# Where the MLP norm's scale and offset are applied, and the order of five queues: a change to a fused two-branch block on one Trainium2 core

## The reference, cut to what matters

```python
xn = _layernorm(x)                       # x: 1 x 4096 x 256
s  = linear_attention(xn)                # 16 heads of 32, softmaxed q and k, decay mask, _ln, W_out
for l in range(2):                       # the local branch, layer l
    h = shift_token(x)
    q, k, v = split(h @ wqkv)            # 8 heads of 64
    q, k = rotary_xpos(l2norm(q) * qs, l2norm(k) * ksc)
    x = x + local_attention(q, k, v) @ wo        # windows of 128, look back one window
    h = shift_token(x)
    h = (h - mu) / sqrt(var + 1e-5) * lg + lb    # the MLP norm
    a, g = split(h @ w1 + b1)
    x = x + (a * gelu(g)) @ w2 + b2
out = x0 + s * silu(x)
```

## Time and profile before

| | us |
|---|---|
| runs | 2031.31, 2036.61, 2037.25 |
| median | 2036.61 |
| profiled execution | 2033.74 |
| its span | 2031.7 |
| TensorE busy | 1933.6 |
| VectorE busy | 1733.0 |
| ScalarE busy | 1169.2 |
| GpSimd busy | 1015.4 |

### The profile page before, as it was taken

How to read it: one execution, slowest core, us unless ns; L and a number is a source line. 1 busy time by engine, 2 the same in 40 slices (tenths; PEclk the granted TensorE clock), 3 DMA queues, 4 the chain that set the end, 5 groups by cost and what they waited for, 6 DMA issues and landing times.

```text
span 2031.7 us, 49195 instructions
## 1 busy us (share of the span) xinstructions
PE 1933.6 (95%) x15282; PEld 1663.3 (82%) x15282; DVE 1733.0 (85%) x5322; ACT 1169.2 (58%) x2798; POOL 1015.4 (50%) x1005
## 2 busy tenths in 40 slices
PE   5899999999999999999999999999999999999997
PEld 3788888888888888888888888888888888888886
DVE  5788888988888988888876898888899888899885
ACT  3456655655655665655654566566566556556553
POOL 2455455656455655455543455444455453455451
PEclk8799999999999999999998999999999999999998
DMA  5010010010000010000120111110111110111100
GB/s 196 17 32 20 26 31 19 30 31 18 29 27 25 25 31 19 30 26 29 53 86 17 43 32 41 34 31 28 41 31 41 34 31 28 41 32 40 34 28 24
DMA packets 81153, 72.76 MB, mean 36 GB/s; under 512 B 13485, under 2 KB 74345, under 8 KB 81097
## 3 DMA queue, kind: packets, MB, share of 16 engines
q1 hardware_dynamic: 81096, 72.05, 11.7%
HBM read 42.64 MB, written 16.78 MB: 29 GB/s over the span
## 4 chain that ended last, share of the span: by engine, by line
PE 65%; DVE 21%; issue 9%; ACT 2%; POOL 1%; DVEq 1%; SPq 0%; DMA 0%; ACTq 0%; POOLq 0%
PE bank L1477 31%; PE bank L1482 20%; PE bank L1489 10%; PE bank L1534 3%; DVE prob L1022 2%; DVE rot L1377 2%; DVE rot L1387 2%; DVE sq_sum L1351 2%; DVE gel L1241 1%; DVE hid L1260 1%; DVE prob L1041 1%; DVE kT L1213 1%; ACT kT L782 1%; POOL small_y L658 1%; DVE rot_scale L1245 1%
## 5 line engine op out<-in xcount | busy, mean ns | idle before, releaser
L1477 PE MATMUL bank<-hT_n,w_s 128*128 128x128 f32 x3072 | 405.3, 283 | 1.1 <-ACT hT_n L782 0.5
L1477 PEld LDWEIGHTS bank<-hT_n,w_s 128*128 128x128 f32 x3072 | 370.3, 194 | 26.2 <-issue 21.4
L813 ACT ACTIVATE prob<-prob,row_min 128x256 f32<-128x256 f32 x512 | 256.3, 503 | 165.0 <-DVE row_min L1022 164.4
L1482 PE MATMUL bank<-wqkv_s,xT 128*128 128x512 f32 x1152 | 322.0, 416 | 7.3 <-DVE xT L1218 4.7
L701 POOL TENSOR_TENSOR rot_other<-raw,rot_t 128x256 f32<-128x256 f32 x256 | 187.4, 763 | 245.7 <-ACT raw L782 245.7
L658 POOL TENSOR_TENSOR inv_norm<-sq_clip,half_neg 128x8 f32<-128x8 f32 x128 | 242.7, 1906 | 80.2 <-DVE sq_clip L1354 80.0
L1482 PEld LDWEIGHTS bank<-wqkv_s,xT 128*128 128x128 f32 x1152 | 209.9, 193 | 56.4 <-DVE wqkv_s L1195 6.4
L1022 DVE CUSTOM_DVE_ANT_0 prob<-bank,table,inv_norm 128x256 f32<-128x256 f32 x512 | 226.2, 478 | 2.9 <-issue 2.9
L1477 PE MATMUL bank<-w_s,hid 128*128 128x256 f32 x768 | 202.2, 386 | 1.2
L782 ACT ACTIVATE pT<-bank 128x512 f32<-128x512 f32 x256 | 143.4, 604 | 69.4 <-PE bank L1489 69.2
L1534 PEld LDWEIGHTS bank<-kT,qT 64*128 64x128 f32 x1536 | 100.2, 187 | 68.1 <-DVE row_min L1022 34.2
(11 more groups left out here) (184 smaller groups left out, 4297.3 us busy)
## 6 DMA issues: line engine op xcount, KB each, us to landing
k_prev<-k_carry SPq DMA_DIRECT2D x32, 224.0 KB, 2.5
x_s<-in_L_attn_x SPq DMA_DIRECT2D x32, 128.0 KB, 2.0
rot_s<-in_rotary SPq DMA_DIRECT2D x64, 64.0 KB, 2.0
rows_normalised<-xh SPq DMA_DIRECT2D x32, 128.0 KB, 1.7
y_n<-rows_normalised SPq DMA_DIRECT2D x32, 128.0 KB, 2.1
x_between_layers<-x SPq DMA_DIRECT2D x32, 128.0 KB, 1.7
s_between_passes<-s_out SPq DMA_DIRECT2D x32, 128.0 KB, 1.7
x_s<-x_between_layers SPq DMA_DIRECT2D x32, 128.0 KB, 2.0
```

The lines of the kernel that those rows point to most:

```text
L813: ins = act.activation(prob[:, h, :], prob[:, h, :], ACT.Exp, bias=row_min[:, c:c + 1], scale=-1.0, accum_out=row_sum[:, c:c + 1])
L1477: return pe.matmul(out, lhsT, rhs, start=first, stop=last)
L1482: ins = pe.matmul(out, halved(left[:, a]), halved(right[:, b]), start=first and n == 0, stop=last and n == 2)
```

## The change

Five things, in the words of the code.

- ScalarE's copy of `hT_n` becomes two activations (Identity) of 128 x 128 with a scale (gain) and a bias (offset) per partition. Both folds, `b1_s` and the setup events of them are gone; the gates take b1 from `cols`, and the first MLP matmuls of a layer wait for the load of w1 instead of its scaling.
- `norm3` and the store of its rows (SyncE's `store_rows`) move from the end of an iteration into the next one: `norm3` before `scores("b1")`, the store before the DMAs of `k_prev`.
- VectorE: `scores("a0")` before y_n. In odd iterations the sum of squares before p. The low half la before cos. The rotary's addition in two halves; in odd iterations kadd and lb between them. In odd iterations `norm1` and `hidden_tail` behind ql.
- TensorE, even iterations: `state_sum` ahead of `mlp_out(0, 2)` and `turn_q`. `turn_k` directly behind the output projection, ahead of `mlp_out(2, 4)` and the transposes of `go`. ScalarE's copy of k goes before that of `go` accordingly, and its zeroing of kT in the first window of a layer moves forward.
- Where a layer begins: ScalarE cuts the q weights before it copies the transposed rows, and in layer 1 the k and v weights are cut later, on ScalarE after the copy of q and on VectorE after `scores("a1")`.

```diff
-        b1_s = [sb(f"b1_s{l}", [P, 2 * HC]) for l in range(LAYERS)]
...
+        def b1_cols(l):
+            return cols[:, NORM_ROWS + l * 2 * HC:NORM_ROWS + (l + 1) * 2 * HC]
...
+                if 1 <= i.low < NW:
+                    store_rows(i)
                 if mix is not None:
                     sp.wait_ge(mix_pool.sem, mix_pool.at("ksmear", mix))
...
-                if i.low + 1 < NW:
-                    store_rows(i.back(-1))
...
                     act.wait_ge(mlp_pe.sem, mlp_pe.at("ht", m))
-                    copy(hT_n[:, :, :], mlp_bank[1][:, 0:D].rearrange("p (c t) -> p c t", c=DC))\
-                        .then_inc(mlp_act.done("ht"), 1)
+                    gain, offset = norm_cols(6 + 2 * layer(m)), norm_cols(7 + 2 * layer(m))
+                    for c in range(DC):
+                        ins = act.activation(hT_n[:, c, :], mlp_bank[1][:, c * P:(c + 1) * P], ACT.Identity,
+                                             bias=offset[:, c:c + 1], scale=gain[:, c:c + 1])
+                    ins.then_inc(mlp_act.done("ht"), 1)
...
-            def fold(l):
-                dve.wait_ge(setup_pe.sem, setup_pe.at(f"b1_{l}", ONCE))
-                dve.tensor_tensor(b1_s[l][:, :], mlp_bank[0][:, 0:2 * HC], cols[:, at:at + 2 * HC], ALU.add)\
-                   .then_inc(setup_dve.done(f"b1_{l}"), 1)
-                for c in range(DC):
-                    ins = dve.tensor_scalar(w1_s[:, c, :], w1_s[:, c, :], norm_cols(6 + 2 * l)[:, c:c + 1],
-                                            None, ALU.mult)
...
+            def add_other(u, part, name):
+                half = slice(part * E, (part + 1) * E)
+                dve.tensor_tensor(rot[:, half], rot[:, half], rot_other[:, half], ALU.add).then_inc(proj_dve.done(name), 1)
...
+                if a is not None:
+                    scores("a0", a, att_bank[0])
                 if y is not None:
                     dve.wait_ge(mix_pool.sem, mix_pool.at("yrstd", y))
...
+                if 1 <= i.low < NW:
+                    norm3(u)
                 if a is not None:
                     scores("b1", a, att_bank[0])
                 if one is not None:
+                    square_sums(u)
                     dve.wait_ge(mix_pe.sem, mix_pe.at("p", one))
...
-            def fold(l):
-                pe.wait_ge(w1_loaded, 16 * W1_DMAS * (l + 1))
-                for j in range(2 * HC):
-                    for c in range(DC):
-                        ins = mm(mlp_bank[0][:, j:j + 1], w1_s[:, c, j * P:(j + 1) * P],
-                                 norm_cols(7 + 2 * l)[:, c:c + 1], c == 0, c == DC - 1)
...
                     hidden(m, mlp_bank[0], 2, 4, 2).then_inc(mlp_pe.done("ga"), 1)
-                    if one is None:
-                        mlp_out(m, 0, 2)
+                if two is not None:
+                    state_sum(two, 0)
+                    state_sum(two, 1)
+                if m is not None and one is None:
+                    mlp_out(m, 0, 2)
...
                     out_projection(a, att_bank[1])
+                if u is not None:
+                    turn_k(u)
                 if m is not None and two is not None:
                     mlp_out(m, 2, 4)
```

115 lines of the change are left out of this document (54 added, 61 removed).

## The result

The changed kernel takes 2019.4 us (median of 5 runs, 2018.2 to 2022.7) against 2036.6 (5 runs, 2029.5 to 2039.0). The ratio is 0.9926 with a 95% interval of 0.9904 to 0.9949: 10 to 20 us less. The forecast was 1993 us and a range of 1963 to 2015. The sign is right, the size is not, and the time lies outside the range.

The account below looks back on a forecast made before the run. TensorE, busy 95% of the span, was taken as the bound, with VectorE (85%) close behind and the only engine waited for. Once-only savings -30.5, layer 1's loop -23.4 and layer 0's +10 gave -44: 2036.6 to 1993 us, range 1963 to 2015.

Parts of the forecast that it names:

- The second, 8.8 + 3.2: Second fold: its one-column matmuls go, 8.8 us, and the slow-clock stretch behind it, 3.2 us; together 12.0 us saved.
- The first, 8.05 + 2.0: First fold: its one-column matmuls go, 8.05 us, plus 2.0 us from the slow clock behind it; 10.0 us saved.
- The rival of 2032 us: Half the folds' 17 us returns as waits, layer 1 gains nothing, layer 0 loses 10 us; chance 0.05.
- The pair of activations: ScalarE's replacement for the hT_n copy: holds it 0.27 us longer per unit, ends 0 and 0.376, mostly beside other work.
- -15.5: Start to iteration 2: 3.0 us from cutting q first, 2.5 from iteration 1's waits, 10.0 from the first fold.
- I take 3.0 us in all, ends 0 and 8: Where layer 1 begins: row_min's wait goes, kT's shrinks, the slow stretch may shorten; 3.0 us saved.
- I take all 23.4 us, ends 8 and 28: Layer 1's loop: all three of TensorE's waits for VectorE go, 23.4 us saved.
- +10 forecast: Layer 0's loop: 0.4 us from the even and 0.3 from the odd iteration, over 15 pairs; 10 us slower.
- p is some 0.4 us later, and with it tanh, the exponentials and the gelu by 0.15 to 0.3 us: Layer 0's odd iterations: norm3 (0.3 us) and the sum of squares (1.3) before p, where VectorE idles 1.19.
- The rival of VectorE's pace: VectorE sets both loops' pace, each pair 2.2 us longer over 30 pairs, the kernel slower at 2072 us; chance 0.07.
- the own case: Whole kernel: the prediction's main forecast of 1993 us, spanning 1979 to 2007; chance 0.48.
- the main term: The loops' forecast; called wrong if kT's wait is below 9 us in layer 0 or 8.5 or more in layer 1.

Follow-up runs that it names:

- e4: The kernel before with only the folds taken out, ScalarE applying gain and offset in two activations, all orders as before: 2012.0 us, ratio 0.9887.
- e1: The changed kernel with the sums of squares of odd iterations back behind p: 1998.1 us, ratio 0.9814.
- e7: The changed kernel with the squares back behind p and both halves of the rotary addition ahead of kadd: 1992.6 us, ratio 0.9810.
- e8: The changed kernel with squares behind p, both rotary halves ahead of kadd, and four of eight state additions ahead of qT's low half: 1971.1 us, ratio 0.9704.
- e13: The changed kernel with squares behind p, both rotary halves ahead of kadd, and state sums back behind the q transposes: 1975.7 us, ratio 0.9702.
- e17: The kernel before without folds, plus scores a0 and la early, early k transposes and state sums, four state additions ahead of qT's low half: 1969.2 us, ratio 0.9682.
- e6: The changed kernel with the first four of VectorE's eight state additions ahead of qT's low half in even iterations: 2001.1 us, ratio 0.9845.
- e5: The changed kernel with the state sums back behind the q transposes in even iterations: 2008.0 us, ratio 0.9880.
- e16: The kernel before without the folds, with scores a0 ahead of y_n and la ahead of cos on VectorE: 1984.0 us, ratio 0.9740.
- e2: The changed kernel with the first four gated columns ahead of the k half of the rotary addition in odd iterations: 2036.4 us, ratio 1.0013.
- e3: The changed kernel with both halves of the rotary addition ahead of kadd in odd iterations: 2010.3 us, ratio 0.9881.

## Why the prediction was wrong, and what was right

Of the 33 us between the forecast and the profile, 16.7 lie in layer 1's loop, 10 where layer 1 begins and 6.8 in layer 0's loop. The sign is that of the folds: the orders by themselves made the kernel slower.

**The folds.** 22.0 us forecast, 23.2 measured (e4). The second, 8.8 + 3.2, measured 11.7. The first, 8.05 + 2.0, shows 6.7 up to iteration 2 and 1.0 behind it; the rest of e4's gain, 2.8 us, is in the tail behind iteration 63, and belongs to no term. The rival of 2032 us, by which half of that time would come back as waits for other engines, is out. The pair of activations was given 0.27 us with 0.376 as its upper end; it takes 0.80 as one record where the copy took 0.38, 0.42 more, and costs a pair 0.04 to 0.08 us.

**The start.** -15.7 against -15.5, and the agreement is luck. The q cut gave 3.3 (forecast 3.0). In iteration 1 prob's wait fell from 2.9 to 1.6 us and mix_work's rose from 2.2 to 3.3: 0.2 us instead of 2.5. With the squares back behind p (e1) they are 2.9 and 1.0, so the squares are what moved the wait. A new wait of 1.95 us for kT stands before the rows of iteration 2. In all TensorE's idle time fell by 1.6 us, where 5.5 were forecast; its busy time fell by 14.1, of which 8.05 are the fold and 6.0 go with a mean granted clock of 0.92 instead of 0.85, where 2.0 were forecast.

**Where layer 1 begins.** The step "I take 3.0 us in all, ends 0 and 8" failed. The folds alone give 135.4 us from iteration 31 to 35, the change takes 142.1: 6.7 us more, outside its ends. 4.1 of them are idle time of TensorE (7.9 to 12.0), 2.6 busy time. In the view of TensorE's waits of the change, 980 to 1080 us, which answers to the earlier trace rows:

```profile
PE bank L1502 <- DVE mix_work L1406: 3.8, 2, 2.1
PE bank L1495 <- DVE wqkv_s L1205: 3.4, 2, 2.3
PE bank L1490 <- DVE hid L1259: 2.4, 2, 1.2
PE bank L1490 <- ACT gel L930: 2.1, 2, 1.5
```

row_min's and kT's 4.8 us are smaller or gone, 2.3 us of wqkv_s are what the text called "a little later" and gave no price, and the two loops' new waits are larger here than in the loops. With the squares and the split undone, TensorE idles 6.2 to 6.9 us in the stretch (e7, e8, e13) against e4's 7.9: the parts that the step credited save 1.0 to 1.7 us of waiting. The rest is busy time, 126.0 to 129.5 us in these three for nearly the same work, at a mean granted clock of 0.99 in e7 and e13 and 0.96 in e8.

**Layer 1's loop.** The step that failed is "I take all 23.4 us, ends 8 and 28"; measured 5.1 over 14 pairs. The 1.56 us a pair that it stands for can be had: e17 has the moves that were credited, with e6's edit, and is 1.55 below e4. That the two agree to a hundredth is luck, since TensorE's idle time fell by only 1.12 us a pair (a new wait for mix_work, 0.64, stays) and 0.43 are busy time, records that follow each other more closely. What failed is that the other moves of the same change were walked for layer 0 alone. The sum of squares and the split stand in layer 1's odd iterations as well, and cost 0.91 us of the 1.14 between the change and e17; 0.23 lie in what else e7 and e17 differ by.

**Layer 0's loop.** +10 forecast, +16.8 measured, 0.7 against 1.12 us a pair. The even part, state sums ahead of the q transposes, was right in its mechanism and mis-sized: 0.4 forecast, 0.9 measured (e5), and the wait for kT grew to 11.7 us in the stretch of the earlier trace rows, not the 15 that was named. The odd part has one false step: "p is some 0.4 us later, and with it tanh, the exponentials and the gelu by 0.15 to 0.3 us". It was 1.1 us. From start to start, the norm's product holds VectorE for 0.44 us (given 0.3) and the squares with their clip for 1.68 (given 1.3; the clip takes 0.52 instead of 0.17), and VectorE comes to this place 0.24 us later than before. And no one was asked to wait for the gelus: before, they ended 0.35 us before TensorE came for their bank (434.77 + 1.14 = 435.91 against 436.26 in the kernel before), so 0.3 us later was free. They came 0.7 later, and TensorE came 0.46 earlier, which makes 0.8. The delay is 0.87 us, 0.70 of it idle. Undone, the move is worth 1.13 us (e1).

**The k half.** It was given 0.6 us. It takes 1.12 in the iteration shown, since GpSimd's product runs until 0.55 us before its end, and hid came late, a wait the prediction did not have. The rival of VectorE's pace, 7%, had the mechanism and 2.2 us a pair; it set its own decision point at 1.0, and layer 0 passed it with 1.12. Layer 1 did not. The spread of the own case, 1979 to 2007, does not follow from the stated ends: half of them, added up, reach from about 1969 to 2013. The measured 2019.4 lies outside either.

**What the profile was to show.** No one-column matmuls, no more loads of ScalarE's tables (126 in both), row_min near nothing, no oT in layer 1, full clock at the first MLP matmuls of iteration 34 and VectorE idling 0.86 us before la: all so. kT in layer 0 over 9 and in layer 1 under 8.5: so, and both tests of the main term passed while it was wrong by 17 us. They asked whether old waits went, not whether new ones came.

Not settled: the odd iterations of e13 are 0.64 us longer than those of e16 in layer 0. Between them lie the new place of the next rows' norm, of the last gated columns, and the addition in two instructions; they were not tried one by one.

## What to carry to other kernels

Removing a wait by moving an instruction forward paid about what the wait was (0.51, 0.59 and 0.46 us of a pair of layer 0, for waits of 0.46, 0.42 and 0.61, and they added), but everything that jumps ahead of a producer must be priced for every consumer behind it on all engines, down to one that today is early by a few tenths. An idle time on an engine is free only as far as its end stays: a change that also brings the engine behind it 0.46 us earlier takes that much of the room. The view of waits shows idle time alone, 0.70 us where the delay was 0.87. Two engines whose instructions hold each other up make order a matter of phase: the same instruction cost 0.72 or 1.43 us by where GpSimd's stood, so such a move is tried, not summed. And compare lengths of periods, not whole times: they show 0.1 to 0.2 us in 60, where whole times here show 5 in 2000.

## What the runs showed of the hardware that was not expected

Not every operation of VectorE was longer beside GpSimd. The gated columns, which read one operand from TensorE's bank, take 1.12 us in e2 beside GpSimd's products and 332 to 350 ns each over the whole changed kernel; the low halves of qT and kT take 675 to 693. The rotary addition, with both operands in SBUF, spreads from 679 to 1587 ns, and the mean-and-scale of h_n, with one, from 342 to 761. In the changed kernel (ns, minimum, median, maximum):

```profile
L1266 DVE TENSOR_TENSOR rot<-rot,rot_other x128: 679/694/1587, 23.7 to 1966.0; 128x512 f32<-128x512 f32 x128
...
L1223 DVE TENSOR_TENSOR kT<-bank,kT x64: 678/692/693, 33.5 to 1971.9; 128x512 fp32r<-128x512 f32 x64
...
L1259 DVE SCALAR_TENSOR_TENSOR hid<-bank,cols,gel x256: 332/335/350, 90.3 to 2012.8; 128x128 f32<-128x128 f32 x128
...
L1322 DVE TENSOR_SCALAR h_n<-x,mv_h,small_h x64: 342/682/761, 73.6 to 2004.0; 128x128 f32<-128x128 f32 x64
```

It goes the other way too. GpSimd's second product for the gate, which begins in the changed kernel while the k half runs, takes 1.60 us in each of 12 odd iterations of layer 0, against 1.27 in the kernel before:

```profile
L735 POOL TENSOR_TENSOR gate<-gate,mix_work x12: 1600/1604/1607, 186.5 to 863.4; 128x512 f32<-128x512 f32 x12
```

GpSimd's long root of few columns did not block VectorE: in e3 both halves take 1.29 us together in the middle of its 2.63 (a record of GpSimd's is rough in its length):

```profile
428.26 1.29 DVE L1266 TENSOR_TENSOR rot<-rot,rot_other 128x512 f32<-128x512 f32 x2
...
427.10 2.63 POOL L659 TENSOR_TENSOR inv_norm<-sq_clip,half_neg 128x8 f32<-128x8 f32 x1
```
